# Attention with 16-wide heads: value products turned to a row a query, normalized there and turned back; layer norm rows on VectorE

## The reference

```python
h = _layernorm(x, ln1_w, ln1_b)
q, k, v = qkv(h)                              # 16 heads of 16
attn = softmax(mask(einsum('bhtd,bhsd->bhts', q, k) * scale))
sa = einsum('bhts,bhsd->bhtd', attn, v)       # then (B, T, 256)
x = x + sa @ proj_w + proj_b
h = _layernorm(x, ln2_w, ln2_b)               # the same with keys and values of the context
x = x + ca @ out_w + out_b
x = x + gelu(_layernorm(x, ln3_w, ln3_b) @ mlp1_w + mlp1_b) @ mlp2_w + mlp2_b
```

## Time and profile before

| | |
|---|---|
| median of 3 runs | 1760.25 us (1759.25 to 1762.0) |
| profiled execution: its own time | 1761.67 us |
| its span, which all views count from | 1759.9 us |
| TensorE busy | 1629.7 us (93%) |
| VectorE, ScalarE, GpSimd busy | 963.5, 1024.7, 721.0 us |
| mean granted clock of TensorE | 0.973 |

### The profile page before, as it was taken

The page is one execution under the profiler, slowest core; times in us unless marked ns, Lnnn a source line. Parts: engine busy times, 40 slices in busy tenths (PEclk is TensorE's granted clock), DMA queues, the critical chain, the costliest instruction groups (busy, mean ns, idle before and its releaser), DMA issues.

```text
span 1759.9 us, 37106 instructions
## 1 busy us (share of the span) xinstructions
PE 1629.7 (93%) x13752; PEld 1384.0 (79%) x13752; DVE 963.5 (55%) x2440; ACT 1024.7 (58%) x2794; POOL 721.0 (41%) x1273
## 2 busy tenths in 40 slices
PE   5899999999989999999999899999999878988876
PEld 5788888887788888888888788878888766766666
DVE  5655544445546546544445547543445687666643
ACT  3556656556725556656566725555566765666771
POOL 5865333333233545333333233433334356646311
PEclk9999999999999999999999999999999898999988
DMA  4521200001101101100001101100012100110000
GB/s 133 169 85 42 72 15 14 17 25 50 50 28 37 40 2 55 59 15 14 28 19 52 44 27 51 52 15 14 15 38 64 32 14 24 34 35 22 4 7 21
DMA packets 39411, 67.45 MB, mean 38 GB/s; under 512 B 7296, under 2 KB 13408, under 8 KB 39232
## 3 DMA queue, kind: packets, MB, share of 16 engines
q1 hardware_dynamic: 39232, 65.06, 12.0%
HBM read 57.67 MB, written 5.54 MB: 36 GB/s over the span
## 4 chain that ended last, share of the span: by engine, by line
PE 79%; DVE 7%; ACT 5%; issue 3%; POOL 2%; DMA 2%; SPq 1%; DVEq 0%; POOLq 0%; ACTq 0%
PE pG L957 48%; PE pG L1083 11%; PE pS L957 10%; PE pO L957 9%; DVE PT L1351 2%; ACT L1252 1%; DMA PT<-PT 1%; SPq L943 1%; DVE KF L1338 1%; ACT hid_lo_f L1252 1%; ACT P L1213 1%; ACT PT L1226 1%; PE pG L1125 0%; DVE bn L1267 0%; DMA x<-x_in 0%
## 5 line engine op out<-in xcount | busy, mean ns | idle before, releaser
L1429 POOL TENSOR_SCALAR P<-P,rinv 112x375 f32<-112x375 f32 (+1 forms) x640 | 323.4, 516 | 513.0 <-DVE rinv L1344 509.1
L1213 ACT ACTIVATE P<-pS,nmax 112x375 f32<-112x375 f32 (+1 forms) x640 | 305.8, 491 | 208.9 <-DVE nmax L1320 208.7
L957 PE MATMUL pG<-hT_hi,W 128*128 128x224 f32 (+1 forms) x1408 | 330.4, 312 | 31.0 <-POOL hT_lo L1489 17.7
L957 PEld LDWEIGHTS pG<-hT_hi,W 128*128 128x128 f32 x1408 | 246.9, 198 | 41.3 <-issue 15.3
L1320 DVE TENSOR_REDUCE nmax<-pS 112x1 f32<-112x375 f32 (+1 forms) x448 | 226.3, 547 | 94.3 <-PE pS L957 93.6
L1226 ACT ACTIVATE PT<-pG 125x336 f32<-125x336 f32 (+1 forms) x448 | 207.9, 466 | 115.7 <-PE pG L1083 113.0
L1083 PE MATMUL pG<-ident,P 112*125 112x112 f32 (+1 forms) x1472 | 242.1, 278 | 15.6 <-POOL P L1429 7.1
L957 PE MATMUL pG<-src,W 128*128 128x376 f32 x1120 | 244.0, 348 | 2.8 <-DVE hid_hi_f L1297 2.8
L1083 PEld LDWEIGHTS pG<-ident,P 112*125 112x125 f32 (+1 forms) x1472 | 201.9, 177 | 51.7 <-issue 9.8
L957 PE MATMUL pG<-W,src 128*125 128x512 f32 x840 | 234.5, 412 | 1.8 <-DVE hid_hi_f L1297 1.8
L957 PE MATMUL pG<-hT_lo,W 128*128 128x224 f32 (+1 forms) x704 | 212.7, 302 | 0.0
(11 more groups left out here) (94 smaller groups left out, 2590.4 us busy)
## 6 DMA issues: line engine op xcount, KB each, us to landing
wraw<-wts SPq DMA_DIRECT2D x120, 256.0 KB, 2.6
src<-ctx_split SPq DMA_DIRECT2D x64, 282.0 KB, 3.0
ctx_split<-hid_lo_t SPq DMA_DIRECT2D x8, 564.0 KB, 3.6
V<-ctxT SPq DMA_DIRECT2D x8, 376.0 KB, 4.2
V<-wts SPq DMA_DIRECT2D x8, 256.0 KB, 3.7
PT<-PT SPq DMA_DIRECT2D x64, 28.0 KB, 1.9
bo_b<-bo SPq DMA_DIRECT2D x10, 112.0 KB, 2.7
out<-x SPq DMA_DIRECT2D x8, 112.0 KB, 1.9
```

Of the source, the lines that this page charges most:

```text
L957: return nc.tensor.matmul(o, l, r, start=first, stop=last)
L1213: ins = act.activation(o, pS[U % 4][0:T, i * n:(i + 1) * n], ACT.Exp, bias=nmax[:, r, i:i + 1], accum_out=rsum[:, r, i:i + 1])
L1429: ins = pool.tensor_scalar(o, o, rinv[:, r, i:i + 1], st.nscale, ALU.mult, ALU.mult)
```

## The change

- In the small stages VectorE only copies pO to ao_raw. A new piece `ta` turns the copy on TensorE (four transposes), so that a query is a row and the sum of a head is one number in it. VectorE takes the reciprocal of 112 x 16 sums and multiplies 112 x 256 products into ao_rows. A new piece `tb` turns these back (two transposes); ScalarE adds the bias and rounds to AOT_hi, VectorE subtracts to AOT_lo. The four DMAs and the GpSimd steps are gone.
- The result is dense: two tiles of 128 rows for the 256 columns, so `wo` has six matmuls, and its weights (chunks 2 and 3 of items 27 and 28) are fetched without padding, by 8 DMAs a chunk. The two bias vectors are laid out dense by 32 DMAs of 16 x 1 (`bias`).
- `ve` and `hn` of all 80 layer norms move from GpSimd to VectorE; `rstd` stays.
- `fill`, `tail` and the numbers of `duration` follow. In the tail `wo` now stands behind ff2 3.

```diff
 def fill(s, b, i):
         if b > 1:
-            out.insert(1, Ev("wo", s, b - 3) if b > 2 else Ev("wo", 4, B - 1))
             out.append(Ev("v", s, b))
+            out.insert(1, Ev("ta", s, b - 2))
+            out.insert(3, Ev("tb", s, b - 2))
...
+    if b and i == 1:
+        out.append(Ev("ta", s, b - 1))
+    if b and i == 2:
+        out.insert(1, Ev("tb", s, b - 1))
+        out.append(Ev("wo", s, b - 1))
...
 def tail(s, held, scored):
-        out = [held[0]] + scored + [Ev("ff2", s, 0), held[1], Ev("lnt", ff.ln, B - 2), Ev("ff2", s, 1), Ev("ff2", s, 2),
-                                    Ev("wo", s, B - 1), Ev("ff2", s, 3), Ev("lnt", ff.ln, B - 1)]
+        out = [held[0]] + scored + [Ev("lnt", ff.ln, B - 2), Ev("ff2", s, 0), held[1], Ev("ff2", s, 1), Ev("ta", s, B - 1), Ev("ff2", s, 2),
+                                    Ev("tb", s, B - 1), Ev("ff2", s, 3), Ev("wo", s, B - 1), Ev("lnt", ff.ln, B - 1)]
...
+    for s in (5, 6):
+        task("sp", Ev("bias", s), not_before=200.)
...
-        inverse, scaled = PT[:, 0:CHUNK], PT[:, CHUNK:2 * CHUNK]
+        ao_raw, ao_rows = PT[:, CHUNK:2 * CHUNK], PT[0:T, 0:C]
...
+        def packed(n):
+            return CHUNKS[n][0] in (27, 28) and CHUNKS[n][1] > 1
...
 @block.sync
+                    if packed(n):
+                        for t in range(2):
+                            for r in range(4):
+                                rows = slice(64 * t + 16 * r, 64 * t + 16 * r + 16)
+                                sp.dma_start(view[rows, 0:C], wts[CHUNKS[n][0], 32 * r:32 * r + 16, e.i * WQ + t * C:e.i * WQ + (t + 1) * C]
+                                             ).then_inc(wraw_in[buf], 16)
...
+                elif e.kind == "bias":
+                    wait(sp, consts_in, 64)
+                    for t in range(2):
+                        for r in range(4):
+                            rows = slice(64 * t + 16 * r, 64 * t + 16 * r + 16)
+                            for k in range(2):
+                                sp.dma_start(bias_c[rows, s - 5, k:k + 1], bsm_sb[32 * r:32 * r + 16, 3 * s - 13, t + 2 * k:t + 2 * k + 1]
+                                             ).then_inc(bias_in, 16)
...
-                elif e.kind == "shift":
-                    sp.wait_ge(sums_inv, m + 1)
-                    wait(sp, ao_split, m)
-                    for r in range(0, 128, 32):
-                        sp.dma_start(scaled[r:r + 16, :], inverse[r + 16:r + 32, :]).then_inc(shifted, 16)
...
 @block.tensor
-                            wait(pe, ao_scaled, mask_no(s, b))
+                            wait(pe, ao_out, mask_no(s, b))
...
+                    for n in range(2 if st.small else sh.NT):
+                        t, step = (ao_tiles(e)[n], WQ) if st.small else (n, C)
...
+                elif e.kind == "ta":
+                    pe.wait_ge(ao_out, mask_no(s, b) + 1)
+                    for t in range(4):
+                        ins = nc.tensor.transpose(g[0:T, t * 128:(t + 1) * 128], ao_raw[:, t * T:(t + 1) * T], ident[:, :])
+                elif e.kind == "tb":
+                    pe.wait_ge(ao_normed, mask_no(s, b) + 1)
+                    for k in range(2):
+                        ins = nc.tensor.transpose(g[:, k * T:(k + 1) * T], ao_rows[:, k * 128:(k + 1) * 128], ident[0:T, 0:T])
...
 @block.scalar
+                elif e.kind == "tb":
+                    wait(act, bias_in, 512)
+                    for k in range(2):
+                        ins = act.activation(AOT_hi[:, ao_tiles(e)[k], :], g[:, k * T:(k + 1) * T], ACT.Identity,
+                                             bias=bias_c[:, s - 5, k:k + 1])
...
 @block.vector
+                dve.tensor_scalar(ve[:, r:r + 1], mv[:, r, 1:2], EPS, None, ALU.add).then_inc(ln_ve, 1)
...
-                    dve.reciprocal(inverse, pO[:, 0:4 * T]).then_inc(sums_inv, 1)
...
-                        dve.wait_ge(shifted, 64 * (mask_no(s, b) + 1))
-                        dve.tensor_tensor(scaled, scaled, pO[:, 0:4 * T], ALU.mult).then_inc(ao_scaled, 1)
+                        dve.tensor_copy(ao_raw, pO[:, 0:4 * T]).then_inc(ao_out, 1)
...
+                elif e.kind == "ta":
+                    dve.reciprocal(sums_inv[:, :], heads[:, :, 16]).then_inc(ao_inv, 1)
+                    dve.tensor_tensor(ao_rows.rearrange("p (h d) -> p h d", d=16), heads[:, :, 0:16],
+                                      sums_inv[:, :].rearrange("p (h d) -> p h d", d=1).broadcast_to([T, H, 16]), ALU.mult).then_inc(ao_normed, 1)
+                elif e.kind == "tb":
+                    for k in range(2):
+                        ins = dve.scalar_tensor_tensor(AOT_lo[:, ao_tiles(e)[k], :], g[:, k * T:(k + 1) * T], bias_c[:, s - 5, k:k + 1],
+                                                       AOT_hi[:, ao_tiles(e)[k], :].bitcast(F32), ALU.add, ALU.subtract)
...
+                elif e.kind == "hn":
+                    dve.wait_ge(ln_rstd, stat_no[s, b])
+                    dve.tensor_scalar(hn[:, n % 2, :], x[:, b, :], mv[:, r, 0:1], rstd[:, r:r + 1],
+                                      ALU.subtract, ALU.mult).then_inc(ln_h, 1)
...
 @block.gpsimd
-                elif e.kind == "ao":
-                    for t in range(4):
-                        ins = pool.tensor_scalar(o, o, bsm_sb[:, 2 if s == 5 else 5, t:t + 1], 1.0, ALU.add, ALU.mult)
-                    pool.tensor_scalar(AOT_hi[:, 0:4, :], sc, 1.0, 1.0, ALU.mult, ALU.mult).then_inc(ao_rounded, 1)
-                    pool.tensor_tensor(AOT_lo[:, 0:4, :], sc, AOT_hi[:, 0:4, :].bitcast(F32), ALU.subtract).then_inc(ao_split, 1)
...
-                    pool.tensor_scalar(ve[:, r:r + 1], mv[:, r, 1:2], EPS, None, ALU.add).then_inc(ln_ve, 1)
...
-                elif e.kind == "hn":
-                    pool.wait_ge(ln_rstd, stat_no[s, b])
-                    pool.tensor_scalar(hn[:, n % 2, :], x[:, b, :], mv[:, r, 0:1], rstd[:, r:r + 1],
-                                      ALU.subtract, ALU.mult).then_inc(ln_h, 1)
```

More of the change, by code:

```diff
@@ L273, in fill @@
         out += [Ev("ffg", s, 0, 2 * i), Ev("ffg", s, 0, 2 * i + 1)]
-    if b == 0 and i in (1, 2):
-        out.append(Ev("lnt", st.ln, B - 4 + i))
-    if b == 1 and i == 0:
-        out.append(Ev("lnt", st.ln, B - 1))
-    if i == 3:
-        out.append(Ev("wo", s, b - 1) if b else Ev("wo", 5, B - 1))
+    if (b, i) == (0, 1):
+        out.append(Ev("ta", 5, B - 1))
+    if (b, i) == (0, 2):
+        out.insert(1, Ev("tb", 5, B - 1))
+        out += [Ev("lnt", st.ln, B - 2), Ev("wo", 5, B - 1)]
+    if (b, i) == (0, 3):
+        out.append(Ev("lnt", st.ln, B - 1))
+    if b and i == 1:
[3 more added lines that the diff above has]
+        out.append(Ev("wo", s, b - 1))
     return out
@@ L360, in duration @@
         if k == "wo":
-            return 1.42 if st.small else 2.83
-        return dict(q=.68, qk=1.36, k=.86, lnt=.23, ffg=1.24, ffa=1.24, ff2=2.83)[k]
+            return .75 if st.small else 2.83
+        return dict(ta=.48, tb=.27, q=.68, qk=1.36, k=.86, lnt=.23, ffg=1.24, ffa=1.24, ff2=2.83)[k]
     if engine == "act":
@@ L378, in duration @@
         if k == "ao":
-            return .62 if st.small else .55
-        return dict(inv=.62, ql=.36, w=.58, stat=.65, k=.55, qk=.72, norm=.15, wo=1.55, ff2=1.55, lnt=.78, ctx=.5, ffa=1.65, ffg=1.1)[k]
+            return .62 if st.small else .6
+        return dict(ta=.75, tb=.68, hn=.42, ql=.36, w=.58, stat=.75, k=.55, qk=.72, norm=.15, wo=1.6, ff2=1.6, lnt=.78, ctx=.5, ffa=1.65, ffg=1.1)[k]
     if k == "norm":
         return 1.2 if st.self_ else .6
-    return dict(hn=.5, lnt=1.1, k=1.65, ao=2.9, ones=.8, rstd=.85, ctx=1.9, mask=1.2)[k]
+    return dict(lnt=1.15, k=1.65, ones=.8, rstd=.6, ctx=2.2, mask=1.)[k]
 def context_pieces(pieces, s, b):
@@ L453, in plan @@
         elif e.kind == "wo":
-            needs += [("pool" if STAGES[s].small else "dve", Ev("ao", s, b, o)) for o in range(SHAPES[s].NO)]
+            needs += [("dve", Ev("tb", s, b))] if STAGES[s].small else [("dve", Ev("ao", s, b, o)) for o in range(2)]
+        elif e.kind == "ta":
+            needs.append(("dve", Ev("ao", s, b)))
+        elif e.kind == "tb":
+            needs.append(("dve", Ev("ta", s, b)))
         elif e.kind == "lnt":
-            needs.append(("pool", Ev("hn", s, b)))
+            needs.append(("dve", Ev("hn", s, b)))
         elif e.kind in ("ffg", "ffa"):
@@ L488, in plan @@
             task(*evicted(e), ("pe", e))
-        elif e.kind in ("wo", "ff2"):
+        elif e.kind in ("wo", "ff2", "ta"):
             task("dve", e, ("pe", e))
+        elif e.kind == "tb":
+            task("act", e, ("pe", e))
+            task("dve", e, ("act", e))
         elif e.kind == "lnt":
@@ L652, in program @@
     assert [e for e in order["act"] if e.kind == "ao"] == [e for e in aos if e.s < 5]
-    for engine, kind in (("dve", "inv"), ("sp", "shift"), ("pool", "ao")):
-        assert [e._replace(kind="ao") for e in order[engine] if e.kind == kind] == [e for e in aos if e.s > 4]
```

(16 more changed lines are left out.)

97 lines of the change are left out of this document (53 added, 44 removed).

## The result

Over five runs each the changed kernel takes 1752.75 us (1751.48 to 1755.3) and the kernel before 1762.0: ratio 0.9951, 95% interval 0.9936 to 0.9965, some 9 us faster. Forecast were 1733, in a range from 1714 to 1748. The profiled execution has a span of 1750.7 us against 1759.9.

What follows compares the result with a forecast made beforehand. TensorE bounds the wide layers; its 72.5 us of idle in the small stages are latency on an in-order engine. Terms -19.5, -2.5, -3, -9, -5, +10, +1.5 sum to -27.5 us: 1733 us, range 1714 to 1748.

Steps and rivals of the forecast that it cites:

- the price of the norms on VectorE: ve and hn on VectorE: +1.5 us at the start, ends 0 and 3, and no cost in the wide stages.
- elsewhere in the wide stages hn and ve on VectorE cost nothing: Wide stages after the start: TensorE is the cover, 0 us; without cover 56 norms would cost 28 us.
- GpSimd's chain gets shorter by as much: Start: VectorE gets about 2 us of hn and ve before the first scores, GpSimd loses as much; +1.5 us in all.
- the term of +10 us for the queue: SyncE queue near 212 us: 32 small bias DMAs take 17 us, delay a weight chunk, TensorE loses 10 us; ends 3, 13.
- Stage s = 6: Batches of s = 6: 22.6 us each, a gain of 2.9; with batch 0, 19.5 us, plus 2.5 up to the last batch.
- Stage s = 5: Stage s = 5: VectorE stays near the bound and loses 1.3 us a batch, 9 us gained over 7 batches; ends 4, 13.
- the whole part on the small stages: Terms for s = 6, its last batch, s = 5 and tail: -19.5, -2.5, -3, -9, -5 us.
- The last batch: Batch 7 of s = 6: of TensorE's 4.78 us wait for the multiply, 3 us gained; ScalarE would be next late.
- The tail: Tail: ff2 3 ahead of wo shortens 15.8 us before the feed-forward to 10.9; gain 5 us, ends 3 and 7.
- VectorE keeps the small stages: Rival, small stages: transposes' round trips expose 2 us a batch, not 0.8; 1748 us, from 1741 to 1756; chance 0.19.
- GpSimd slowed by hn: Rival, wide stages: hn on VectorE slows GpSimd through shared SBUF interfaces, 22 us back, 1755 us; chance 0.03.
- The slower rival: Rival, wide stages: hn makes VectorE stand for rstd, 1 us for each of 56 norms, 1789 us; chance 0.05.

Runs made afterwards that it cites:

- a_bias: The changed kernel with both bias vectors laid out dense before launch and fetched by one DMA instead of 32: 1737.8 us, ratio 0.9878 to the kernel before.
- t_normsp: a_bias_tail with ve and hn of all 80 norms back on GpSimd: 1720.05 us, ratio 0.9771 to the kernel before.
- a_bias_normsp: a_bias with ve and hn back on GpSimd, the tail as in the change: 1722.8 us, ratio 0.9792 to the kernel before.
- best_last: t_normsp with the last hn on VectorE and useless transposes in the tail (1716.5 us), plus such transposes in the last s = 6 batch: 1720.4 us.
- a_warm: a_bias with useless transposes in TensorE's idle time in the tail, 26 before the last norm's transposes, 16 before the last gate pieces: 1733.6 us, ratio 0.9848.
- b_norms: The kernel before with only ve and hn moved from GpSimd to VectorE: 1773.7 us, ratio 1.0084 to the kernel before.
- a_bias_tail: a_bias with the tail's last output projection again ahead of ff2 3, as in the kernel before: 1733.7 us, ratio 0.9851 to the kernel before.

## Why the prediction was wrong

The step that failed is the price of the norms on VectorE. The prediction had +1.5 us at the start, nothing in the wide stages, and for s = 5 the 0.55 us a batch of `hn` and `ve` in VectorE's sum, 3.9 us over seven batches. Moved back, they gave 13.6 and 15.0 us in two kernels: by the means of the nine profiles 6.8 at the start, 2.9 in the wide work and 4.5 in s = 5. So s = 5 was sized rightly, and the start and the claim that "elsewhere in the wide stages hn and ve on VectorE cost nothing" were wrong. In "GpSimd's chain gets shorter by as much" I had looked at what one engine does for a norm, and not at the chain of the context split, which needs GpSimd, VectorE and a write in turn: it became what TensorE waits for. Why the wide work loses 2.9 us is open.

The second is a size: the term of +10 us for the queue measured 17.5 between the two profiles, 17.0 between the changed kernel and a_bias, and 15 in the medians. The links held, and three of them were short. The burst took 20.6 us and not 17. The 17 were 0.53 us a DMA, under the median of 0.59 in the earlier trace rows, which alone gives 18.9; the burst's own DMAs have that median, 0.589 us, and some are longer, up to 1.03. The transfer behind it took 3.2 us for 2.6, so ScalarE stood 15.0 us for 10.6 and TensorE 15.25 for 10. Then came 2.2 us that I hadn't counted at all: behind the wait the granted clock was 0.50 for 4 us, and four matmuls took 1.60 us where the same four ahead of it had 0.89. The far end of the term, 13, had no room for that.

**Stage s = 6** was right in mechanism and nearly in size: a batch of 22.9 us for 22.6. **Stage s = 5** came to -7.5 for -9; without the norms the prediction's sum of VectorE's operations is 3.57 - 0.62 - 0.2 - 0.42 - 0.5 = 1.83 us less a batch, 12.8 over seven, and t_normsp and a_bias_normsp gave 12.1 and 12.9.

With the norms on GpSimd the whole part on the small stages measured -37 to a sum of its terms of -39. That this is so near is in part luck. Against the kernel before, a_bias_normsp has -12.9 in s = 5 (for -9), -20.4 in the seven batches of s = 6 (-22), +1.6 in the last batch (-3), -5.4 in the tail (-5), +2.4 behind it (0), and -2.6 ahead of the small stages, where the two kernels do nearly the same work.

**The last batch** gave nothing for the 3 us. "ScalarE would be next late" was right: in place of the wait of 4.78 us for the multiply stand waits for ScalarE (2.17, 2.03 and 2.23 us among them), and all of the gain went there. best_last shows that bound.

**The tail** gave 6.6 for 5 up to the gate pieces. I then counted the feed-forward behind them as unchanged; it lost 2.9 us, 2.8 of them in the 48 matmuls that ran at 0.51 of the clock at first. a_warm shows the cause for that window: with filler in the idle times of 3.29 and 2.08 us the clock stays at 1.00. One idle time right ahead is not enough to explain it, as the kernel before has 2.23 us there and full clock; it has 0.27 us where the changed one has 3.29. How much it is worth in the median stays open, as the executions of one kernel differ by as much elsewhere.

Of the rivals, neither "VectorE keeps the small stages" (1748) nor "GpSimd slowed by hn" (1755) is what happened, though the time lies near them. VectorE's new operations cost what was taken: the copy 618 ns, reciprocal 257, multiply and hn 424 each. GpSimd's normalization of the probabilities between 80 and 1375 us has a mean of 521 ns in both traces, but its small operation `rstd` has 643 ns after and 568 before:

```profile
L1514 POOL TENSOR_SCALAR P<-P,rinv 112x375 f32<-112x375 f32 (+1 forms) x602 | 307.0, 521 | 572.6 <-DVE rinv L1408 572.4
...
L1541 POOL TENSOR_TENSOR rstd<-ve,mhalf 112x1 f32<-112x1 f32 x53 | 34.1, 643 | 207.2 <-DVE ve L1333 207.1
```

The two halves of hT are longer as well (hT_hi 461 ns for 422, hT_lo 751 for 722), and b_norms shows the same (rstd 644, hT_hi 462, hT_lo 756). All this is some 8 us of GpSimd's time over the wide stages. So the contention that the Trainium skill ("GPSIMD Engine Reference", section on its specifications) allows for would be small in this trace, far from the rival's 22 us; whether it has a part in the 2.9 us of the wide work, no run tells. The slower rival, VectorE standing for `rstd`, is small too: 6.7 us of idle over all 80 hn.

Four points stay open: whether work, plan or order makes the first context write late; what costs 2.9 us in the wide work; how b_norms' 14.5 us divide between the norms and a stage s = 6 that varies by itself; and why a_bias_tail and a_warm gained some 3 us more in the median than their profiles show at the edit.

## What to carry to other kernels

Before a burst of small DMAs is put on a queue, multiply their count by at least the median issue of that shape in the trace (0.59 us here; the burst had 0.645) and look at what the queue's next chunk is for: here 32 copies of 64 bytes cost 15 to 17.5 us, and one dense transfer made them nothing. When work moves to another engine and the order is planned anew, the sum of what each engine gains and loses is not the price: look for chains that pass through both engines and a transfer, as the context split here, and at when each link starts. One profile is too little to price an edit of a few us. Idle time ahead of a long run of matmuls can be paid twice; filler has to stand in every gap of such a run, and it pays for itself only where TensorE would stand and is what the end waits for.
